# Experts: sort the tokens by their pair of experts and compute only the two that were chosen, on 91 pages of 128 slots

## The reference

```python
xn = (x - mu) * rsqrt(var + EPS) * gamma + beta
logits = einsum('bsd,de->bse', xn, Wr) + br
top_vals, top_idx = top_k(logits, 2)
w_full = softmax(top_vals) placed at top_idx, zero for the other six experts
for e in range(8):                     # D = 128, H = 256
    h = gelu(xn @ W1[e] + b1[e])       # 128 -> 256
    y += (h @ W2[e] + b2[e]) * w_full[..., e]
x = x + y
```

## Time and profile before

| | |
|---|---|
| time, median of 3 | 1126.28 us (1126.01 to 1126.47) |
| profiled execution | 1126.91 us, span 1125.1 us |
| mean granted TensorE clock | 0.769 |
| PE busy | 942.1 us (84%) |
| DVE, ACT, POOL busy | 805.4 (72%), 557.3 (50%), 167.4 (15%) us |
| DMA | 39.70 MB in 58323 packets, mean 35 GB/s |

### The profile page before, as it was taken

How to read it: one execution, slowest core, us unless ns; L and a number is a source line. 1 busy time by engine, 2 the same in 40 slices (tenths; PEclk the granted TensorE clock), 3 DMA queues, 4 the chain that set the end, 5 groups by cost and what they waited for, 6 DMA issues and landing times.

```text
span 1125.1 us, 21842 instructions
## 1 busy us (share of the span) xinstructions
PE 942.1 (84%) x6990; PEld 643.4 (57%) x6990; DVE 805.4 (72%) x2993; ACT 557.3 (50%) x1568; POOL 167.4 (15%) x309
## 2 busy tenths in 40 slices
PE   0976777777777777777747999999999999999998
PEld 0754444444444444444425776667677766776765
DVE  4355777777777777777735778877777888777785
ACT  1233444444444444444414666666666666666664
POOL 5501111111111111111111001111010111100000
PEclk9995555555555555555557999999999999999999
DMA  7900111011111111111020000000000000000000
GB/s 203 163 3 20 39 38 37 28 34 36 37 37 33 37 37 37 32 33 33 28 70 19 1 29 29 28 28 28 0 28 28 28 28 28 28 16 12 9 9 19
DMA packets 58323, 39.70 MB, mean 35 GB/s; under 512 B 4191, under 2 KB 57636, under 8 KB 58276
## 3 DMA queue, kind: packets, MB, share of 16 engines
q1 hardware_dynamic: 55971, 36.83, 12.3%
q0 software_dynamic: 656, 2.11, 0.6%
q10 hardware_dynamic: 1674, 0.49, 0.2%
HBM read 26.12 MB, written 13.30 MB: 35 GB/s over the span
## 4 chain that ended last, share of the span: by engine, by line
PE 53%; DVE 27%; ACT 12%; issue 6%; DMA 2%; POOL 0%; SPq 0%; DVEq 0%; POOLq 0%
PE pb L680 13%; PE pb L699 12%; PE pb L594 9%; DVE CC L1111 6%; ACT tanh_c L831 5%; DVE h L1113 4%; ACT S L827 4%; DVE glo L1214 3%; PE pb L626 3%; PE pb L642 3%; PE pb L687 3%; DVE Gw L1210 2%; DVE ys L1040 2%; ACT GC L829 2%; PE pb L653 2%
## 5 line engine op out<-in xcount | busy, mean ns | idle before, releaser
L594 PEld LDWEIGHTS pb<-h,vp 128*128 128x128 bf16 x3840 | 142.2, 106 | 214.0 <-DVE h L1113 211.5
L594 PE MATMUL pb<-h,vp 128*128 128x32 f16 x3840 | 170.3, 191 | 94.0 <-DVE h L1113 86.0
L891 ACT ACTIVATE Gl<-pb,vcols 128x512 f32<-128x512 f32 x256 | 162.3, 685 | 144.8 <-PE pb L680 144.8
L1210 DVE TENSOR_TENSOR Gw<-Gl,pb 128x1024 f32<-128x1024 f32 x128 | 155.8, 1217 | 103.1 <-PE pb L687 92.6
L1214 DVE TENSOR_TENSOR glo<-Gw,ghi 128x1024 fp32r<-128x1024 f32 x128 | 157.7, 1232 | 0.0
L827 ACT ACTIVATE S<-pb 128x64 f32<-128x64 f32 x256 | 58.2, 227 | 162.4 <-PE pb L594 162.4
L871 ACT ACTIVATE ghi<-Gw 128x1024 fp32r<-128x1024 f32 x128 | 135.1, 1055 | 1.7 <-DVE Gw L1210 1.7
L568 PE MATMUL pb<-xbuf,us 128*128 128x256 f32 x198 | 118.2, 703 | 0.6 <-ACT xbuf L813 0.6
L680 PE MATMUL pb<-xhi,w1hi 128*128 128x512 f32 x256 | 115.6, 452 | 0.0
L1111 DVE TENSOR_TENSOR_SCAN CC<-S,GC 128x64 f32<-128x64 f32 x256 | 74.4, 291 | 51.7 <-ACT GC L829 46.2
L831 ACT ACTIVATE tanh_c<-CC 128x32 f32<-128x32 f32 x256 | 59.0, 231 | 93.5 <-DVE CC L1111 93.5
(11 more groups left out here) (223 smaller groups left out, 1470.1 us busy)
## 6 DMA issues: line engine op xcount, KB each, us to landing
adjn<-in_adj SPq DMA_DIRECT2D x32, 256.0 KB, 2.7
x_d<-x2s SPq DMA_DIRECT2D x33, 128.0 KB, 1.8
y_d<-ys SPq DMA_DIRECT2D x33, 128.0 KB, 1.8
yr<-y_d SPq DMA_DIRECT2D x16, 256.0 KB, 2.8
x2r<-x_d SPq DMA_DIRECT2D x16, 256.0 KB, 3.1
out<-outb SPq DMA_DIRECT2D x16, 256.0 KB, 2.3
X<-in_x SPq DMA_DIRECT2D x4, 912.0 KB, 17.5
aW<-in_L_gnn_W SPq DMA_DIRECT2D x2, 640.0 KB, 10.8
```

The costliest lines, as they stand in the source:

```text
L594: return mm(o, vp[p][:, q, :], h[:], start=False, stop=True, skip_group_check=True)
L891: a = av(Gl[e % 2][:, c, :], PB[2 * (e % 2) + c][:], ACT.Gelu, bias=eb1[:, e, c:c + 1])
L1210: v.tensor_tensor(Gw[e % 2][:], Gl[e % 2][:], bc(PB[5][:].unsqueeze(1), [P, 2, 4 * P]), ALU.mult).then_inc(gw_ready, 1)
```

## The change

The expert stage is replaced. Tokens are routed first, in eight batches of 1024 (`NF`): residual, statistics, the power on POOL (`norm_scale`), normalisation on ACT, an upper and a lower f16 half of the normalised token, transposes, logits, and the two largest. From the two indices DVE makes the code of the pair, one of 28 (`NQ`), and a one-hot row of 28; PE counts, in one PSUM bank that is kept through all batches, how many tokens of the same pair came before (`places`, `advance`), and DVE reads each token's slot from it (`assign`). POOL sends a row of 1040 bytes for each token (x, both halves, the two weights, the token's number) to its slot in DRAM (`xs_d`, a region for each pair), with eight indirect DMAs for a batch (`send`). After the last batch DVE and PE make a table of the pages: row of `xs_d`, the two experts' addresses, and which slots are valid. Then come 91 pages of 128 slots (`PAGES`), written out without a loop: SP loads a page from an address in a register (`values_load` fills registers from a table in SBUF), PE transposes it (2) and does 16 matmuls of layer 1 and 14 of layer 2, all 128 columns wide and all with an expert's address from a register, ACT and DVE do GELU and the halves in f16, DVE combines the two experts with their weights and adds x, and POOL stores the rows at their tokens' places by an indirect DMA.

Other parts: the constants' first load is cut from 1452 to 420 columns and the rest follows later (`kons`); W1 and W2 are loaded by SP behind the first adjacencies, not by POOL at the start; the weights' splitting in f16, with scales that are powers of two, and the biases are computed by POOL in `prepare`, a piece in each half group of the recurrence, whose POOL loop is written out; PE's and ACT's first four groups are written out and have four small matmuls each more; 3.7 MB of zeros are written to `xs_d`; CC moves from SBUF to a PSUM bank, and the adjacency's transposes from bank 6 to bank 4.

```diff
+PAIRS = [(a, b) for a in range(E) for b in range(a + 1, E)]
+NQ = len(PAIRS)
+REG = B * T + P
+PAGES = (B * T + NQ * (P - 1)) // P
...
-            CC = sb("CC", [P, B, 2], where=rec)
...
+        CC = PB[7][:, 0:2 * B].rearrange("p (b k) -> p b k", k=2)
...
-            sp.dma_start(const[:], io["consts"]).then_inc(ld_const, 16)
+            sp.dma_start(const[:], io["consts"][:, 0:C_N]).then_inc(ld_const, 16)
...
+            sp.dma_start(wst[:], io["L1_ffn_W1"].rearrange("e d h -> d e h")).then_inc(ld_w, 16)
+            for c in range(2):
+                sp.dma_start(w2st[:, :, c, :], io["L1_ffn_W2"][:, c * P:(c + 1) * P, :].rearrange("e h d -> h e d")).then_inc(ld_w, 16)
...
+            sp.dma_start(xs_d.rearrange("(q r) w -> r q w", r=REG)[0:P], zrow[:].unsqueeze(1).to_broadcast([P, NQ, ROW])).then_inc(rows_zeroed, 16)
...
+            sp.wait_ge(table_ready, 1)
+            for i in range(NBUF):
+                sp.wait_ge(rows_sent[i], 16 * NT * (NF // NBUF))
+            rows = None
+            for t in range(PAGES):
+                if t % 4 == 0:
+                    n = min(4, PAGES - t)
+                    _, rows = nc.values_load_multi_w_load_instructions(
+                        row_i[0:1, t:t + n], engines=[mybir.EngineType.SP], min_val=0, max_val=NQ * REG - P,
+                        skip_runtime_bounds_check_because="each row is the start of a region plus at most 8064 rows of its 8320")
+                if t >= XR:
+                    sp.wait_ge(out_ready, t - XR + 1)
+                sp.dma_start(Xp[t % XR][:], xs_d[bass.ds(rows[t % 4], P), :]).then_inc(page_loaded[t % XR], 16)
...
-            for dst, src in experts:
-                pool.dma_start(dst, src).then_inc(ld_wb, 16)
...
+            def prepare(G, part):
+                if G < 4:
+                    squares(G, part)
...
+            def norm_scale(F):
+                k = F % 2
+                pool.wait_ge(m_aggr, F + 1)
+                tp.tensor_scalar(nm_m[k][:], mv_m[k][:, :, 0], -1.0, None, ALU.mult)
+                link(tp.tensor_scalar(ve_m[k][:], mv_m[k][:, :, 1], LN_EPS, SC ** -2, ALU.add, ALU.mult))
+                link(pw(rs_m[k][:], ve_m[k][:], half8[:], ALU.pow))
+                pw(nb_m[k][:], nm_m[k][:], rs_m[k][:], ALU.mult).then_inc(nb_ready, 1)
+            def send(F):
+                pool.wait_ge(slot_ready, F + 1)
+                pool.wait_ge(lo_ready, F + 1)
+                pool.wait_ge(hi_ready, F + 1)
+                pool.wait_ge(tok_ready, F + 1)
+                for i in range(NT):
+                    pool.indirect_dma_start(xs_d, bass.IndirectOffsetOnAxis(slot[F % NBUF][:, i:i + 1], 0), stg[F % NBUF][:, i, :], None).then_inc(rows_sent[F % NBUF], 16)
+            norm_scale(0)
+            for F in range(1, NF):
+                norm_scale(F)
+                send(F - 1)
+            send(NF - 1)
+            for t in range(PAGES):
+                pool.wait_ge(out_ready, t + 1)
+                pool.indirect_dma_start(out_rows, bass.IndirectOffsetOnAxis(out_i[t % 4][:, 0:1], 0), outb[t % 4][:], None,
+                                        bounds_check=B * T - 1, oob_is_err=False).then_inc(out_stored[t % 4], 16)
...
-            with pe.Fori(0, NGRP // 4) as it:
+            def four_groups(it, once):
...
+                        if once and s in (0, 1, 2):
+                            if q4 == 0 and s == 0:
+                                pe.wait_ge(ld_w, 48)
+                                pe.wait_ge(beta_ready, 1)
+                            for n in ((0,), (1,), (2, 3))[s]:
...
+            def places(F):
+                oh = oneh[F % 2]
+                pe.wait_ge(oneh_ready, F + 1)
+                m = mm(rank_b[:, 0:NT * NQ], trih[:], oh[:].rearrange("p i q -> p (i q)"), start=False, stop=True, skip_group_check=True)
+                for i in range(NT - 1):
+                    n = NT - 1 - i
+                    m = mm(rank_b[:, (i + 1) * NQ:NT * NQ].rearrange("p (n q) -> p n q", q=NQ), onesh[:], bc(oh[:, i:i + 1, :], [P, n, NQ]),
+                           start=False, stop=True, skip_group_check=True)
+                m.then_inc(rank_ps, 1)
...
+            for f in range(4):
+                aggregate(f)
+                project(f)
+            pe.wait_ge(brg_ready, 1)
+            for F in range(NF):
+                if F:
+                    places(F - 1)
+                for u in range(2):
+                    normed_transpose(2 * F + u)
+                if F + 2 < NF:
+                    aggregate(2 * F + 4)
+                    aggregate(2 * F + 5)
+                logits(2 * F)
+                logits(2 * F + 1)
+                if F + 2 < NF:
+                    project(2 * F + 4)
+                    project(2 * F + 5)
+                if F:
+                    advance(F - 1)
+            places(NF - 1)
+            advance(NF - 1)
...
+            def page_transpose(t):
+                pe.wait_ge(page_loaded[t % XR], 16 * (t // XR + 1))
+                if t >= 2:
+                    pe.wait_ge(xT_ready, t - 1)
+                halves = Xp[t % XR][:, P:2 * P].bitcast(F16)
+                for i in range(2):
+                    m = tr(PT[t % 2][:, i * P:(i + 1) * P], halves[:, i * P:(i + 1) * P], identh[:])
+                m.then_inc(xt_ps, 1)
...
+            def layer1(t):
+                _, offs[t] = nc.values_load_multi_w_load_instructions(
+                    off_i[0:1, t, :], engines=[mybir.EngineType.PE], min_val=0, max_val=(E - 1) * EW,
+                    skip_runtime_bounds_check_because="offsets of experts come from a table of constants")
+                pe.wait_ge(xT_ready, t + 1)
+                if t >= 2:
+                    pe.wait_ge(gelu_ready, t - 1)
+                h, x = H[t % 2], xT[t % 3]
+                flat = bt[:].rearrange("p e w -> p (e w)")
+                for j, v in enumerate(offs[t]):
+                    for c in range(2):
+                        o = h[:, (2 * j + c) * P:(2 * j + c + 1) * P]
+                        hi, lo = bass.ds(v + c * P, P), bass.ds(v + (2 + c) * P, P)
+                        mm(o, flat[:, hi], onesb[:], start=(j == 0 and c == 0), stop=False, skip_group_check=True)
+                        mm(o, w1[:, hi], x[:, 0:P], start=False, stop=False, skip_group_check=True)
+                        mm(o, w1[:, lo], x[:, 0:P], start=False, stop=False, skip_group_check=True)
+                        m = mm(o, w1[:, hi], x[:, P:], start=False, stop=True, skip_group_check=True)
+                m.then_inc(l1_ps, 1)
+            def layer2(t):
+                pe.wait_ge(glo_ready, t + 1)
+                if t >= 2:
+                    pe.wait_ge(out_ready, t - 1)
+                flat = bt[:].rearrange("p e w -> p (e w)")
+                gh, gl = ghi[t % 3], glo[t % 3]
+                for j, v in enumerate(offs[t]):
+                    o = Y[t % 2][:, j * P:(j + 1) * P]
+                    mm(o, onesb[:], flat[:, bass.ds(v + 2 * P, P)], start=(j == 0), stop=False, skip_group_check=True)
+                    for c in range(2):
+                        hi, lo = bass.ds(v + c * P, P), bass.ds(v + (2 + c) * P, P)
+                        mm(o, gh[:, 2 * j + c, :], w2[:, hi], start=False, stop=False, skip_group_check=True)
+                        mm(o, gh[:, 2 * j + c, :], w2[:, lo], start=False, stop=False, skip_group_check=True)
+                        m = mm(o, gl[:, 2 * j + c, :], w2[:, hi], start=False, stop=(c == 1), skip_group_check=True)
+                m.then_inc(l2_ps, 1)
+            pe.wait_ge(table_ready, 1)
+            page_transpose(0)
+            for t in range(PAGES):
+                if t + 1 < PAGES:
+                    page_transpose(t + 1)
+                layer1(t)
+                if t >= 2:
+                    layer2(t - 2)
+            layer2(PAGES - 2)
+            layer2(PAGES - 1)
...
+            page_evacuate(0)
+            for t in range(PAGES):
+                gelu(t)
+                if t + 1 < PAGES:
+                    page_evacuate(t + 1)
+                gelu_upper(t)
...
-                        v.tensor_tensor_scan(scan_flat(CC[:]), scan_flat(S[:, 0]), scan_flat(GC[:]), 0.0, ALU.mult, ALU.add).then_inc(cell_ready, 1)
+                        v.tensor_tensor_scan(scan_flat(CC), scan_flat(S[:, 0]), scan_flat(GC[:]), 0.0, ALU.mult, ALU.add).then_inc(cell_ready, 1)
...
+                if F + 1 < NF:
+                    residual(2 * F + 2)
+                    residual(2 * F + 3)
+                    statistics(F + 1)
+                if F:
+                    assign(F - 1)
+                lower_half(F)
+                route(F)
+            assign(NF - 1)
...
+            def combine(t):
+                x, y = Xp[t % XR], PB[2 + t % 2]
+                dve.wait_ge(l2_ps, t + 1)
+                if t >= 4:
+                    dve.wait_ge(out_stored[t % 4], 16 * (t // 4))
```

(13 more changed lines are left out.)

860 lines of the change are left out of this document (482 added, 378 removed).

## The result

The changed kernel takes 1131.46 us (median of 5, 1129.61 to 1134.43) against 1126.36 (5 runs, 1126.01 to 1127.69): ratio 1.0048, 95% interval 1.003 to 1.0067. It is slower by 0.5%; 1077.5 was forecast, with a range of 940 to 1205 and 0.31 for slower.

A forecast was written before the change was run, and what follows sets the result against it. Experts were bound by PE streaming, the new pages by PE's sequencer. First aggregate 577.85 - 4.5 - 8 = 565.4, routing 141, pages 364 and an end of 6 give 1076.3; + 1.8 - 0.6 gives 1077.5 us, range 940 to 1205.

The forecast's parts named there:

- POOL's new work per half group ... falls in its idle time: Recurrence: POOL's added 1.8 to 3.5 us per half group fits its idle 4.6 and 6.3 us.
- the routing, 141 us: From first aggregate to first page: 34 + 93 + 9 + 2 + 3 = 141 us.
- one loop over two batches sets 13.3 us: Routing: a loop of latencies takes 26.6 us for two batches, 13.3 each; seven more batches, 93.
- The pages: Expert stage: PE's sequencer sets 4.0 us a page, 91 pages 364 us; this rival's chance 0.41.
- arithmetic: PE in a page: one fused address instruction ahead of each of 30 matmuls, 30 x 0.08 = 2.40 us.
- Dispatch: PE in a page: issuing ordinary instructions, 64 x 0.019 = 1.22 us.
- The register load: PE in a page: two register loads from SBUF at 0.08 us each.
- Six waits: PE in a page: six waits at 0.08 us each, part of them met early and costing dispatch alone.
- The 0.08: Price in us of one wait or fused address instruction, from the 0.16 difference between two gaps on SP.
- dearer register work: Rival, pages: register work makes a page longer than 4.54 us; at 5.5 the time is 1214; chance 0.26.
- dearer scatters: Rival, routing: 64 scatters above 2.15 us each, POOL's loop bounds; at 2.5 about 1150; chance 0.06.
- CC's gain: Recurrence: tanh reading CC in PSUM saves 0.037 us in each of 256 steps, 9.5 us; 8 taken, range 0 to 9.5.

The follow-up runs named there:

- e4: The changed kernel with CC back in SBUF in place of PSUM: 1141.79 us.
- e6: The kernel before with one more POOL operation, a 128x512 product, at two places (behind rs_y and rs_x), one per half group of the recurrence: 1177.46 us.
- e7: The kernel before with 128x4 powers on POOL at the same places as e6's products: 1127.68 us.
- e10: e9 with the sums of squares of W1 and W2 moved to ACT, in eight ACTIVATEs of 128x512: 1069.16 us, ratio 0.9492.
- e1: The changed kernel with the tanh of batch F-1 ahead of normalise of F in ACT's queue: 1124.64 us, ratio 0.9988.
- e12: The changed kernel with norm_scale one batch earlier on POOL and ACT's queue as it was: 1125.46 us, ratio 0.9984.
- e14: e12 with four buffers for yr and x2r in place of two: 1099.87 us.
- e2: The changed kernel with fixed weight addresses (experts 0 and 1) for every page and no register loads on PE: 1029.41 us.
- e15: e10 with ACT's queue in the changed kernel's order and four buffers for yr and x2r: 1038.79 us, ratio 0.9219.
- e3: The changed kernel with PE loading the registers of four pages at once: 1091.69 us.
- e5: e1 with norm_scale one batch earlier on POOL, ahead of the scatters it stood behind: 1110.36 us.
- e9: The changed kernel with the edits of e3 and e5, and POOL's squares and weight splits in pieces of 128 columns: 1076.08 us, ratio 0.9553.

## Why the prediction was wrong

**The step that failed first: "POOL's new work per half group ... falls in its idle time", and so nothing.** It was costed by POOL's idle time and by who waits for POOL. POOL was indeed never late enough to matter. But some of DVE's operations wait while POOL works on wide operands (1.00 us in L1377 and 1.42 in L1337, which take 0.19 and 0.345 without it), and they are on the chain of the steps or stand ahead of what is: h, and the normalisations ahead of the scan. From first to last store of x_d the recurrence takes 506.2 us, 471.6 before; with the 6.7 us that e4 shows for CC, the work on POOL costs 41 us. DVE's operations take about as much above their medians (41.5), though not each of them lies on the chain. e6 and e7 show it apart from all else: same place, same duration, 1.63 us a group or none. e10, which takes the squares off POOL and leaves the four small products on PE, has groups 1 to 3 at 14.9 us. Beside POOL's products the later operation was held for all that was left of the earlier one (L1377 for 1.00 us beside L502's 1.04); beside e7's powers, which also have two inputs in SBUF, it was not (h 0.21 us beside 1.01), and beside the scaling L564 only for 0.08 us (L1377 0.27 us beside 0.99). No rival of the prediction named such a wait.

**The step that failed second: the routing, 141 us.** Its terms were near one by one: first send 38.0 us behind the first aggregate (34), norm_scale 2.5 (2.4), normalise 3.2 (2.6), last send 9.8 (8.8), landing and load 4.5 (5). A scatter has a pitch of 1.26 us (1.1), eight take 10.7 (8.8). What failed was the claim that one loop over two batches sets 13.3 us: from the first send to the last it is 124 us, and 93 were put. There was another circle, closed in one batch, through ACT's queue, where the tanh of batch F-1 stands behind normalise of F, which waits for norm_scale, which stands behind eight scatters: 18.9 us. Behind it stood three more, of 17.4 (two batches), 15 or more (the two buffers of x2r) and 13.3 (POOL), and the edits alone saved little: e1 -7, e12 -6, but e12 and the buffers together (e14) -31.6. The forecast period was near what the code gives with the circle through POOL's order and the buffers' opened (e14: 14.2); how much of e14's gain is the buffers' is open, as said above.

**The pages: right in sum, by errors that cancel.** PE's issue bounds them, as forecast; the prediction had 4.0 us and the trace has 3.68. By its terms: arithmetic was put at 30 x 0.08 = 2.40 us; there are 22 such instructions, and against the 0.055 us of e2 they add about 0.05 each in layer 1 and 0.04 in layer 2, 1.0 us. Dispatch was put at 64 x 0.019 = 1.22 and the matmuls' streaming at nothing beside it; the two do not overlap so: 32 matmuls at 0.055 are 1.76, and the arithmetic comes on top. The register load was put at 0.16 and is 0.63. Six waits were put at 0.48, of which 0.26 was taken off; the three places where a page waits cost about 0.3. So 1.4 too much for the arithmetic stands against 0.5 too little for the matmuls, 0.5 for the load and 0.1 for the waits, and the near hit is luck. A register address has no price of its own that the trace shows: L992, with a register address and no arithmetic of its own, starts 0.055 us behind L991, as e2's matmuls do with fixed addresses (L975 starts 0.064 us behind L974).

The 0.08 was read from SP's queue, on the footing that an address from a register has one fused arithmetic instruction ahead of it and that a wait directly before goes into that. The trace of before has both (view by line; duration in ns: least, median, longest):

```profile
L327 SPq FUSED_REGOPS  x12: 60/60/66, 610.6 to 977.6; - x12
...
L332 SPq FUSED_REGOPS  x12: 46/46/46, 652.3 to 1009.4; - x12
...
L338 SPq EVENT_SEMAPHORE  x14: 17/17/17, 584.2 to 1010.5; - x14
...
L642 PEldq FUSED_REGOPS  x56: 46/56/93, 630.9 to 1053.8; - x56
```

L327 and L332 have one in each of the 12 iterations inside SP's loop; L328, which shares L327's address, has none. L332's wait has no instruction of its own: its FUSED_REGOPS starts 0.03 us behind the end of the L1219 that it waits for, all 12 times. Of the two waits ahead of L327 one stands alone (L338, 0.017 us). PE's L642 has 56, one for each of the four matmuls that the source writes, in the 14 iterations inside PE's loop. A loop's end on SP is three instructions (L347) of 0.033, 0.045 and 0.050 us. So the difference of 0.16 us between SP's two gaps is the wait and the fused arithmetic of 0.060. What did not carry over to the pages is one arithmetic for every matmul: it is 22 for 30, of 0.032 us (ALU_OP) and 0.044 to 0.046 (FUSED_REGOPS), and a price of about 0.05.

**The range and the chances.** 1131.46 lies inside 940 to 1205, but that is luck too: the range's width was the page's period, and the error came from elsewhere. Of the 0.31 for slower, 0.26 was for dearer register work and 0.05 for dearer scatters; neither made the kernel slower.

**Setup.** The operation L935 of before (L1200 after) starts at 13.1 us; 14.6 was forecast, from 19.10:

```profile
13.12 0.97 DVE L1200 TENSOR_TENSOR adj<-adj,const 25x800 f32<-25x800 f32 x1
```

The first store of x_d comes 6.5 us earlier (98.05 to 91.60; -4.5 forecast). CC's gain was 6.7 us of the 9.5 put as the upper bound: the scan's 11 ns in PSUM come off the tanh's 33, which is 5.6 us in 256 steps; the other 1.1 us was not looked into.

**The end.** Six us were put behind the last page. The last scatter is issued by 1123.6 and the span ends at 1132.6. The profile names what fills the 9 us, an instruction at the end of POOL's program (view by line):

```profile
L99 POOLq DRAIN  x1: 10222/10222/10222, 1122.2 to 1122.2; - x1
```

It begins at 1122.2, lasts 10.2 us and ends at 1132.4. SP's waits for the last stores' landing are over by 1124.9, so 7.5 us come from this instruction alone. e15 has it too (1026.6 to 1036.7), and in the kernel before, which ends in stores from SP, the span ends 2.4 us behind the last store's issue. Why it takes so long is not settled. The pages' window of 350 us contains it, so the fall from 4.0 to 3.68 a page gave more than the 19.8 in the ledger: 29.

What stays open: what of POOL's work holds DVE and what does not (width or kind), DVE's wait of some 2 us in route, and these 7 us at the end. Moving the biases' preparation off POOL, beside which six groups of e15 take 100.9 us (first store of x_d at 363.9, last at 464.8) where six undisturbed ones take 87.9, wasn't tried.

## What to carry to other kernels

Work put in an engine's idle time was not free here (1.63 us a group in e6) where POOL's products of 128x512 ran beside DVE's operations, and was free with powers of 128x4 (e7): ask which operations will run at the same moment as those of the engine on the chain, and price a collision like e6's at up to the whole length of the operation that was there first, as with the 1.06 us that h took beside 1.04 of POOL. A short run like e6, which adds the work to the old kernel where nothing waits for it, gives the price before the change is written. A stage that is moved from under cover into the open is set by its longest circle of waits, so go through every queue once for each batch and list all circles; removing the longest bought only the distance to the next (18.9 us a batch to 17.4 in e1). A register load in a short unrolled body should bring the values of several passes: PE's call cost 0.63 us for two values and 0.67 for eight, and four pages to a call took 39.8 us off (e3).

## What had not been expected

- POOL's product of 128x512 (1.04 us) held a 32-column operation of DVE for 1.06 us; its power of 128x4 (1.01 us) held it not at all (0.21).
- A register load from SBUF on PE costs 0.63 us a call for two values and 0.67 for eight. Matmuls with an address from a register start 0.03 to 0.04 us further apart on average than those without; the cost lies in the arithmetic instructions, 22 for 30 matmuls, and a matmul that takes an address computed before starts 0.055 to 0.064 us behind the last.
- Indirect DMAs of 128 rows from POOL take 0.96 to 0.98 us to issue and 0.30 between two, and land in 2.2 to 2.4 us. The first of a batch takes 1.80 to 1.87 us in the changed kernel, where it comes 5.6 us or more behind norm_scale, and 1.07 to 1.17 in e12, where it comes 0.6 to 0.7 us behind; the stores of the pages take 0.98 after a pause of over 2 us, so it is not the pause alone:

```profile
out<-outb,out_i POOLq DMA_INDIRECT x91, 2.2
...
xs_d<-stg,slot POOLq DMA_INDIRECT x64, 2.4
```

- Two kernels with the same routing, which differ only in other stages (e5 and e9), had batches of 15.5 and 18.5 us on average.
